# Layer-1 attention on one core: the second half of the probabilities turned right behind the scores, the reciprocal taken before the next maximum

## What is computed

```python
q = (_rmsnorm(x @ wq_a.T, q_a_ln_w) @ wq_b.T).reshape(B, S, H, QHD)        # B 8, S 256, H 32, QHD 128
kv = (_rmsnorm(ckv, kv_a_ln_w) @ wkv_b.T).reshape(B, S, H, NOPE + VD)
scores = jnp.einsum('bqhd,bkhd->bhqk', q_full, k_full) * softmax_scale
scores = jnp.where(causal[None, None], scores, jnp.finfo(scores.dtype).min)
attn = jax.nn.softmax(scores, axis=-1)
out = jnp.einsum('bhqk,bkhd->bqhd', attn, v).reshape(B, S, H * VD) @ wo.T
```

## Time and profile before

| | |
|---|---|
| Time, median of 3 runs | 1586.24 us (1585.55 to 1586.72) |
| The profiled execution | 1587.04 us, span of its records 1585.2 us |
| Mean granted clock of PE | 0.958 of full speed |
| PE busy | 1404.6 us of the span |
| VectorE, ScalarE, GpSimd busy | 752.0, 560.1, 622.0 us |

### The profile page before, as it was taken

How to read it: one execution, slowest core, us unless ns; L and a number is a source line. 1 busy time by engine, 2 the same in 40 slices (tenths; PEclk the granted TensorE clock), 3 DMA queues, 4 the chain that set the end, 5 groups by cost and what they waited for, 6 DMA issues and landing times. The chain is left out here.

```text
span 1585.2 us, 25823 instructions
## 1 busy us (share of the span) xinstructions
PE 1404.6 (89%) x8210; PEld 1143.0 (72%) x8211; DVE 752.0 (47%) x1723; ACT 560.1 (35%) x1743; POOL 622.0 (39%) x521
## 2 busy tenths in 40 slices
PE   3999789999999999999996685999999999999950
PEld 0566467777777777777763485999999999999940
DVE  5221466666666666666665674222222222222227
ACT  0232245555555555555553243112111112112114
POOL 0000234444444444444444366534446254471035
PEclk9899989999999999999998897999999999999985
DMA  8032200000000000000003775545656455564337
GB/s 274 0 107 87 100 14 1 14 14 13 13 14 13 13 13 13 13 13 13 14 21 134 291 266 186 190 144 177 211 175 236 141 186 187 183 231 139 106 112 253
DMA packets 66558, 171.50 MB, mean 108 GB/s; under 512 B 6000, under 2 KB 14592, under 8 KB 66192
## 3 DMA queue, kind: packets, MB, share of 16 engines
q0 software_dynamic: 25712, 97.94, 18.5%
q1 hardware_dynamic: 35040, 62.39, 11.8%
q10 hardware_dynamic: 5760, 10.57, 1.9%
HBM read 125.27 MB, written 45.61 MB: 108 GB/s over the span
## 5 line engine op out<-in xcount | busy, mean ns | idle before, releaser
L1593 PE MATMUL bank<-expert_weights,rows_t 128*128 x1872 | 358.7, 347 | 10.6 <-DVE rows_t L1519 10.6
L1593 PEld LDWEIGHTS bank<-expert_weights,rows_t 128*128 128x128 f32 x1872 | 340.3, 189 | 14.2 <-issue 11.0
L926 POOL TENSOR_TENSOR room<-room 128x1024 f32<-128x1024 f32 (+1 forms) x128 | 187.7, 1466 | 343.2 <-DVE room L837 343.2
L896 ACT ACTIVATE room<-bank,room 128x256 f32<-128x256 f32 (+1 forms) x512 | 207.9, 420 | 131.2 <-DVE room L822 131.0
L696 PE MATMUL bank<-room 96*128 (+2 forms) x1024 | 232.4, 347 | 0.3
L1531 DVE TENSOR_TENSOR x_keep<-x_keep,bank 128x400 f32<-128x400 f32 x78 | 44.5, 571 | 303.2 <-ACT x_keep L1470 301.8
L1025 POOL TENSOR_TENSOR expert_weights<-x_keep,expert_weights 128x1600 fp32r<-128x1600 f32 (+2 forms) x49 | 160.2, 3270 | 49.4 <-DMA expert_weights<-w 49.2
L696 PEld LDWEIGHTS bank<-room 96*128 96x128 f32 x1024 | 156.4, 192 | 28.0 <-issue 1.6
L1616 PE MATMUL bank<-expert_weights,act_t 128*128 x702 | 165.6, 389 | 1.0 <-ACT act_t L1475 1.0
L1616 PEld LDWEIGHTS bank<-expert_weights,act_t 128*128 128x128 f32 x702 | 131.5, 188 | 25.6 <-issue 1.3
L1470 ACT ACTIVATE x_keep<-bank 128x400 f32<-128x400 f32 x78 | 39.3, 504 | 298.0 <-PE bank L1593 298.0
(11 more groups left out here) (241 smaller groups left out, 1912.9 us busy)
## 6 DMA issues: line engine op xcount, KB each, us to landing
x_keep<-w POOLq DMA_DIRECT2D x28, 800.0 KB, 4.9
expert_weights<-w POOLq DMA_DIRECT2D x28, 800.0 KB, 6.4
x_keep<-w POOLq DMA_DIRECT2D x14, 768.0 KB, 5.3
expert_weights<-w POOLq DMA_DIRECT2D x14, 768.0 KB, 6.9
rows_by_expert<-room SPq DMA_DIRECT2D x1, 9984.0 KB, 30.0
x_keep<-rows_by_expert SPq DMA_DIRECT2D x39, 256.0 KB, 3.7
results_by_row<-x_keep ACTq DMA_DIRECT2D x39, 256.0 KB, 5.2
room<-wo SPq DMA_DIRECT2D x16, 512.0 KB, 5.2
```

The source lines that it names most:

```text
L896: last = sc.activation(Pr[:, m % 4, hh, 0:w], scores_bank(m)[:, w * hh:w * hh + w], ACT.Exp, bias=nb[:, par, hh:hh + 1], scale=SCALE, accu ...
L926: g.tensor_tensor(pr, pr, rs[:, one[1] % 2].unsqueeze(2).broadcast_to([P, 4, w]), ALU.mult).then_inc(normed, 1)
L1593: last = mm(psum(2 * hf + w)[:, 0:HF], xgT[:, par, of_x, P * k:P * k + P], W[:, ds(off + (of_w * SLOT + (k * 2 + w) * FF + hf * HF), HF)], ...
```

## The change

Five edits, with no work of PE added or removed:

- PE turns the second half directly behind the scores (and values), before the chunk; the first half stays behind the chunk. Values come before the chunk as well.
- VectorE takes the reciprocal for the step before at the start of its step, ahead of the maximum.
- The maximum writes its negative (`negate=True`) straight into the bias; the product with -SCALE and its semaphore fall away. For that SCALE goes into the keys, and the exponential has no scale.
- The low part of the output latents comes one step later (steps 3, 7, 11, 15), behind the rotation; in the emptying steps it comes first.
- ScalarE copies the turned queries between the second and the third of its four exponentials.

```diff
--- before.py
+++ after.py
@@ -557,7 +557,7 @@
                 v.tensor_tensor(part, part, qln.unsqueeze(1).broadcast_to([P, 4, QR]), ALU.mult).then_inc(q_ready, 1)
             for g in range(4):
                 dve.wait_ge(tq, 4 + g + 1)
-                v.tensor_copy(s.KT[0:KC, 512 * g:512 * g + 512], psum(4 + g)[0:KC])
+                v.tensor_scalar(s.KT[0:KC, 512 * g:512 * g + 512], psum(4 + g)[0:KC], SCALE, None, ALU.mult)
 
         @block.gpsimd
         def _(pool):
@@ -619,15 +619,15 @@
     cks = s.carve(2, KVR)
     x_new = s.carve(D)
     qs, Wq = s.qs, s.Wq
-    mx, nb, sm, rs = s.carve(2, 4), s.carve(2, 4), s.carve(2, 4), s.carve(2, 4)
+    nb, sm, rs = s.carve(2, 4), s.carve(2, 4), s.carve(2, 4)
     st, mv = s.carve(6), s.carve(2)
     half = ROPE // 2
     cos = const("cos", "p (k c) -> p k c", k=2)
     sin = const("sin", "p (k c) -> p k c", k=2)
...
@@ -769,25 +769,36 @@
 
             pe.wait_ge(roped, chunks_before(b, m, n, live))
             w.project(bb, qt)
-        if live:
-            w.score(b, m, n)
-            if chunk_here(b, m, live):
-                if m in (5, 13) and not (first and m == 5):
-                    pe.wait_ge(proj_used, b * 2 if m == 5 else b * 2 + 1)
-                w.chunk(b, m, n)
-        three = behind(3)
-        if three and (live or m < 3) and three[1] % 4 == 3:
-            w.values(three[0], three[1] // 4, n - 3)
         two = behind(2)
-        if two and (live or m < 2):
-            if kw(two[1]) == SEQ:
-
+        two = two if two and (live or m < 2) else None
+
+        def turn_second_keys():
+            if two and kw(two[1]) == SEQ:
 
                 if last_entry(b) and (b > LAST or m > 10):
                     pe.wait_ge(k1_out, two[0] * 8 + two[1] - 8)
                 else:
                     pe.wait_ge(q_out, min(n + PRO - 1, 16 * NB) if last_entry(b) else n + PRO - 1)
                 w.turn_p(two[1], n - 2, 1)
+
+        three = behind(3)
+
+        def values_here():
+            if three and (live or m < 3) and three[1] % 4 == 3:
+                w.values(three[0], three[1] // 4, n - 3)
+
+        if live:
+            w.score(b, m, n)
+            values_here()
+            turn_second_keys()
+            if chunk_here(b, m, live):
+                if m in (5, 13) and not (first and m == 5):
+                    pe.wait_ge(proj_used, b * 2 if m == 5 else b * 2 + 1)
+                w.chunk(b, m, n)
+        if not live:
+            values_here()
+            turn_second_keys()
+        if two:
             w.turn_p(two[1], n - 2, 0)
         if chunk_turned(b, m, live):
             w.turn_q(b, m, n)
@@ -796,6 +807,23 @@
         v = nc.vector
         n = b * 16 + m
         behind = parts(b, m, first)
+
+        def low_parts():
+            four = behind(4)
+            if four and four[1] % 4 == 3:
+
+                dve.wait_ge(o_out, four[0] * 4 + four[1] // 4 + 1)
+                half_of = slice(4 * P * (four[1] // 4 % 2), 4 * P * (four[1] // 4 % 2 + 1))
+                v.tensor_tensor(OT[:, LOW, half_of], psum(7), OT[:, HIGH, half_of], ALU.subtract).then_inc(o_low, 1)
+
+        one = behind(1)
+        if one and (live or m < 1):
+            dve.wait_ge(expd, n)
+            if not (isinstance(n, int) and n < 3):
+                dve.wait_ge(normed, n - 2)
+            v.reciprocal(rs[:, one[1] % 2], sm[:, one[1] % 2]).then_inc(summed, 1)
+        if not live:
+            low_parts()
         if m == 3 and live:
 
             if not first:
@@ -816,10 +844,8 @@
         if live:
             par, w = m % 2, kw(m)
             dve.wait_ge(scored, n + 1)
-            v.tensor_reduce(mx[:, par], scores_bank(m)[:, 0:4 * w].rearrange("p (h k) -> p h k", h=4), AX.X,
-                            ALU.max).then_inc(maxed, 1)
-            dve.wait_ge(maxed, n + 1)
-            v.tensor_scalar(nb[:, par], mx[:, par], -SCALE, None, ALU.mult).then_inc(bias_ready, 1)
+            v.tensor_reduce(nb[:, par], scores_bank(m)[:, 0:4 * w].rearrange("p (h k) -> p h k", h=4), AX.X,
+                            ALU.max, negate=True).then_inc(bias_ready, 1)
             if chunk_here(b, m, live):
                 rope(dve, b, m, n)
             if m in (1, 9) and not last_entry(b):
@@ -829,22 +855,12 @@
                 v.tensor_tensor(qs[:, LOW, m // 9], s.QAT[:, ds(tile, 1)].rearrange("p t n -> p (t n)"),
                                 qs[:, HIGH, m // 9], ALU.subtract).then_inc(q_low, 1)
                 tile = None
-        one = behind(1)
-        if one and (live or m < 1):
-            dve.wait_ge(expd, n)
-            if not (isinstance(n, int) and n < 3):
-                dve.wait_ge(normed, n - 2)
-            v.reciprocal(rs[:, one[1] % 2], sm[:, one[1] % 2]).then_inc(summed, 1)
+        if live:
+            low_parts()
         two = behind(2)
         if two and (live or m < 2):
             dve.wait_ge(p_turned, n - 1)
             v.tensor_copy(PT[:, pt_slot(two[1], 0)], psum(5)).then_inc(p_out, 1)
-        three = behind(3)
-        if three and (live or m < 3) and three[1] % 4 == 3:
-
-            dve.wait_ge(o_out, three[0] * 4 + three[1] // 4 + 1)
-            half_of = slice(4 * P * (three[1] // 4 % 2), 4 * P * (three[1] // 4 % 2 + 1))
-            v.tensor_tensor(OT[:, LOW, half_of], psum(7), OT[:, HIGH, half_of], ALU.subtract).then_inc(o_low, 1)
         if tile is not None:
 
             dve.wait_ge(x_summed, tile + 1)
@@ -893,11 +909,11 @@
             par, w = m % 2, kw(m)
             act.wait_ge(bias_ready, n + 1)
             for hh in range(4):
+                if hh == 2 and chunk_turned(b, m, live):
+                    q_leaves(act, m, n)
                 last = sc.activation(Pr[:, m % 4, hh, 0:w], scores_bank(m)[:, w * hh:w * hh + w], ACT.Exp,
-                                     bias=nb[:, par, hh:hh + 1], scale=SCALE, accum_out=sm[:, par, hh:hh + 1])
+                                     bias=nb[:, par, hh:hh + 1], accum_out=sm[:, par, hh:hh + 1])
             last.then_inc(expd, 1)
-            if chunk_turned(b, m, live):
-                q_leaves(act, m, n)
         three = behind(3)
         if three and (live or m < 3) and three[1] % 4 == 3:
             act.wait_ge(pv_done, three[0] * 4 + three[1] // 4 + 1)
```

More of the change, by code:

```diff
@@ L626, in attention @@
     sin = const("sin", "p (k c) -> p k c", k=2)
-    (scored, maxed, bias_ready, expd, summed, normed, chunk_done, roped, q_added, q_turned, q_out, p_turned, p_out,
+    (scored, bias_ready, expd, summed, normed, chunk_done, roped, q_added, q_turned, q_out, p_turned, p_out,
      k1_turned, k1_out, pv_done, o_out, proj_done, proj_used, x_done, q_staged, q_low, v_staged, x_summed,
      stats_done, o_low) = (sem(n) for n in (
-         "scored", "maxed", "bias_ready", "expd", "summed", "normed", "chunk_done", "roped", "q_added", "q_turned",
+         "scored", "bias_ready", "expd", "summed", "normed", "chunk_done", "roped", "q_added", "q_turned",
          "q_out", "p_turned", "p_out", "k1_turned", "k1_out", "pv_done", "o_out", "proj_done", "proj_used",
```

## The result

The changed kernel takes 1542.65 us, median of 4 runs (1538.22 to 1544.69); the kernel before took 1585.98 in the same comparison. The ratio is 0.9723, 95% interval 0.9698 to 0.9747: 2.8% faster, 43 us. The forecast was 1546 (1536 to 1562). The profiled execution is the fastest of the four, 1538.22 us with a span of 1536.4.

The account below looks back on a forecast made before the run. TensorE (PE) was taken to bound layer-1 attention, so only its waits could go: 32.2 us in six inner batches, 2.7 first, 4.4 last, 1 at the stage's end, 40.3 off 1587.04, giving a median of 1546 (1536 to 1562).

Parts of the forecast that it names:

- PE's waits set the gain: Layer-1 attention: PE's queue sets the time, so only its waits can be gained; 40.3 us in all.
- Second half next to the scores: Steps 10, 11, 13, 14, 15: the query turn's wait for ScalarE's copy goes, 0.43 each, 2.15 us per batch.
- Its cover: ScalarE is free when the second half is turned, so its copy ends before the query turn, 0.2 us to spare.
- Reciprocal ahead of the maximum: Earlier normalisation shortens step 0 by 1.34 us, step 1 by 0.49, steps 7 and 8 together by 0.89.
- The circle: Maximum, exponentials, reciprocal, next maximum: 3.9 us with 256 keys, 2.9 to 3.1 with 128; costed at nothing except before projections.
- Before the projections: Steps 4 and 12: projection still waits for the last rotation, so only 0.25 us each, 0.5 per batch.
- The scaling: Product removed from 128 steps on VectorE: under 0.2 us each beside the hand-over, worth only gains already counted elsewhere.
- Low parts: VectorE's low parts one step later: nobody waits; 0 to 0.15 us cost, already in the projection estimate.
- The ends: First batch gains 2.7 us, last batch 4.4, the chain at the stage's end 1.
- A: Rival: only the 56 waits for ScalarE's copy go, the maximum's new wait eats the rest; 24 us, 1562; chance 0.13.
- B: Rival: VectorE's circle is longer than reckoned; 0.75 us more cancels the gain, 1.0 more gives 1601; chance 0.04.
- C: Rival: step 3's VectorE copy of values is held by GpSimd's normalisation, delaying step 5's projection; 8 us, 1554; chance 0.08.

Follow-up runs that it names:

- experiment 1: Kernel before with only TensorE's new order (second half and values ahead of the chunk): batch 79.17 us against 79.04, time 1592.38 beside 1594.24.
- experiment 9: Changed kernel with the output projection in the values' PSUM bank (7) instead of the chunk's (6): batch 71.82 us, time 1563.64 against 1572.88, ratio 0.9672.
- Experiments 2: Kernel before with only the reciprocal moved ahead of the maximum: batch 80.96 us against 79.04, time 1605.11 beside 1594.24.
- 5: Changed kernel with a product by -1 put back between maximum and exponentials, SCALE still in the keys: batch 79.08 us against 73.24.
- 10: Changed kernel with the maximum negated by a second reduce between maximum and exponentials, in place of a product: batch 74.96 us against 73.24.
- experiment 4: Changed kernel with the low parts back at the end of steps 2, 6, 10 and 14: batch 74.94 us, time 1564.72.
- experiment 8: Changed kernel with the projection of steps 5 and 13 behind the scores on TensorE: batch 73.73 us, ratio to the kernel before 0.9761.
- experiment 3: Changed kernel with the query copy behind all four exponentials again: batch 73.47 us, 0.23 more.

## Why the prediction was right, and where it was not

- *PE's waits set the gain.* Right: the attention lost 44.3 us, layer 2 stayed (730.90 and 731.20), and the sum was 40.3. The forecast for the median, 1546 against 1542.65, errs on the same side.
- *Second half next to the scores.* Right in place and a little low in size: 0.49 in step 11 against 0.43, 2.6 in the five steps against 2.15, the largest error of the sum. Its cover held by the 0.17 forecast as 0.2. But "no cost" was right only as part of the whole: by experiment 1 the edit alone gains nothing, since the second half then waits for its normalisation.
- *Reciprocal ahead of the maximum.* Step 0 came to 3.23 (3.20 forecast), step 1 to 3.14 (3.20), steps 7 and 8 to 6.32 (6.32). The circle: from one maximum to the next 591.19 - 588.36 = 2.83 in step 4 (2.9 to 3.1 forecast) and 3.80 from step 8 to step 9, with 256 keys (3.9 forecast).
- *Before the projections.* The maximum at +0.68 instead of +0.75, and steps 4 and 12 at 3.63 and 4.54, where I had 3.76 and 4.59. The wait for the rotation was there, 0.7 and 0.6, and experiment 9 removed it.
- *The scaling.* This is the step that failed, though the sum does not show it. I costed its removal at what step 4 showed, and wrote that the rest of it is "worth only what stands above". I had the hold in the earlier trace rows and the rule beside it, but did not ask what the early reciprocal does to the product if it stays: it sets a normalisation going just before each maximum. Experiments 2, 5 and 10 put the removal at 5.8 us a batch, 4.1 of it the hold. That is its worth with the rest of the change in place; what it gives by itself, in the kernel before, was not run. The sum came out right because I forecast the whole change, in which the operation is gone, and took the lengths of steps from steps without a wait; had the scaling stayed, the forecast of 1569 for the reciprocal alone shows how far off I would have been (80.96 instead of 76.7).
- *Low parts,* costed at nothing: 1.7 a batch by experiment 4. At their old place they make the next maximum late, which I had said, and had not priced. The sum holds even so, since it took most steps at lengths in which nothing waits.
- *What I did not see at all:* step 6 is 0.15 longer (4.04 against 3.88), TensorE standing some 0.2 before the values, which now come right behind the scores. By the code they wait for VectorE's copy of the first half, which ends at 602.59, 0.24 before they start; in experiment 8, where that copy ends well before the scores do, step 6 is 3.87. The profile names no releaser, so this is argued.
- *The ends.* The first batch gained 3.2 (2.7), the last with the end of the stage about 6 (5.4).
- *Rivals.* A fell by step 0 (3.23) and the time: what the early reciprocal gives was not eaten; experiment 1 adds that the 56 waits don't go by themselves. B has a true mechanism: experiment 5 has its circle of 4.6 and its result, no gain, and it is the missing product that keeps the changed kernel from there. But that the amounts agree is luck: of the eight steps that B made longer only step 1 is, and the loss stands in 12, 1, 10, 4, 2 and 6. Its eight terms add up to 5.7, not 5.6.
- *C, by a hair.* Step 3 is 2.75 in the changed kernel as before (2.74), but the copy escaped by little. It starts not 0.09 after the reciprocal, as I had from the earlier trace rows, but 0.22 (588.02 to 588.24), and in each of the six inner batches GpSimd starts only 0.03 later:

```profile
588.24 0.20 DVE L831 COPY room<-room 128x64 f32 x1
588.28 1.06 POOL L942 TENSOR_TENSOR room<-room 128x512 f32<-128x512 f32 x1 [0.69 <-DVE room L824]
```

That such a copy can be held the kernel before shows once, in its first batch: the copy (L803) put out at 233.00 took 0.67 us, where the others took 0.18, and ended 0.06 after GpSimd's normalisation (232.57 to 233.61). So C was missed by luck as much as by the reason given against it.

What stays open: the product taken out of the kernel before with nothing else, and the change without TensorE's order alone, were not run. How the 1.7 us of experiment 10 split between the reduce and its hand-over was not tried, nor an order of ScalarE's that would help both step 0 and step 4.

## What to carry to other kernels

When an edit starts an engine earlier, look at what the other engines do at the new time, not only at who waits for it: here a tiny VectorE tensor_scalar between two SBUF places, and once a small copy, was held until the GpSimd operation beside it ended, and a reduce of the same numbers wasn't. The waits don't show it, since it is not idle time; the longest and the median duration of the line do. Of edits that take a circular wait apart, one alone can show nothing or a loss (0.1 and 1.9 a batch lost here) where all together gain 5.8, so they are judged together. And where two users of one PSUM bank cause the wait that remains, try another bank before another order: here the bank gave 1.4 a batch, and the order lost 0.5.

## What the runs showed of the hardware

- A 128x4 tensor_scalar, 0.17 us by itself, took up to 1.39 us beside GpSimd, and ended 0.02 to 0.05 us after the GpSimd operation in each case in which they overlapped by more than 0.04 us (experiments 2 and 5, and the kernel before); the reduce of the same numbers took 0.156 to 0.159 throughout (experiment 10).
- A reciprocal of 128x4 was not held either: in experiment 3 it began 23 times with more than 0.2 us of GpSimd's sum still to go (at 242.49, say, beside 242.06 to 242.78) and took 0.164 to 0.178, no more than elsewhere.
- The same program takes another time on another chip: the kernel before 1585.98, 1594.24, 1618.93 and 1619.02 us in the four comparisons, on different chips (1594.24 is a single run), the changed one 1542.65 and 1572.88. The changed kernel's attention is the same (586.15 and 585.19); layer 2 takes 731.20 and 765.10, and in the slower run ScalarE stands 35 us once, for something that this core's profile doesn't show (34.4 to 35.0 us in experiments 5, 8 and 9 as well, which have the long times too, and nothing of the kind in experiment 1):

```profile
ACT room L1152 <- remote: 35.0, 1, 35.0
```

It lies outside the change, and the ratio of the two kernels is the same on both chips; what it waits for stayed open.
